# A pre-norm layer in one launch: token rows ahead of code unpacking, the first query step by parts, and the last token block among the feed-forward steps

## The reference, cut to what matters

```python
xn = _layernorm(x)
q = (xn @ Wq + bq).reshape(b, h, t, dh)        # 16 heads of 128
k = (xn @ Wk + bk).reshape(b, t, h, dh).transpose(0, 2, 3, 1)
v = (xn @ Wv + bv).reshape(b, t, h, dh).transpose(0, 2, 1, 3)
weights = softmax(q @ k * scale + causal_mask)
attn = (weights @ v) @ Wo + bo
Wg, Wu, Wd = dequant_nvfp4(...)                # 4-bit codes, a scale per 32 columns
gate, up = xn @ Wg.T, xn @ Wu.T                # 2048 wide
ffn = (gelu(gate) * up) @ Wd.T
return x + attn + ffn
```

## Time and profile before

| | us |
|---|---|
| median of 3 runs | 1270.23 (1269.38 to 1271.47) |
| the profiled execution | 1270.06 |
| its span | 1268.3 |
| PE busy | 1236.2 (97% of the span) |
| DVE busy | 876.2 (69%) |
| ACT busy | 738.6 (58%) |
| POOL busy | 737.8 (58%) |

### The profile page before, as it was taken

One profiled execution on the slowest core, in us unless ns is written; L12 is line 12 of the kernel. 1 busy time (PEld: TensorE's weight loads), 2 busy tenths in 40 slices (PEclk: granted clock), 3 DMA queues, 4 the chain that ended last, 5 costly groups with the idle time before them and its releaser, 6 DMA issues.

```text
span 1268.3 us, 22067 instructions
## 1 busy us (share of the span) xinstructions
PE 1236.2 (97%) x8306; PEld 1119.3 (88%) x8306; DVE 876.2 (69%) x1694; ACT 738.6 (58%) x1533; POOL 737.8 (58%) x772
## 2 busy tenths in 40 slices
PE   8899999999999999999999999999999999999997
PEld 6688888888899999879999998899999879999996
DVE  7687777776577766667667776677667666677765
ACT  3444444444466666657666675566666656666663
POOL 5574455443376676626666663476775527666663
PEclk9999999999999999999999999999999999999999
DMA  5200000000000000110000002010000100000001
GB/s 143 46 14 13 11 10 14 26 2 9 9 26 13 15 13 18 40 49 13 14 26 5 22 13 72 14 55 13 13 22 10 47 26 14 18 22 7 12 5 34
DMA packets 57337, 29.96 MB, mean 24 GB/s; under 512 B 16272, under 2 KB 57232, under 8 KB 57232
## 3 DMA queue, kind: packets, MB, share of 16 engines
q1 hardware_dynamic: 56016, 27.62, 7.9%
q10 hardware_dynamic: 1216, 0.93, 0.2%
HBM read 26.44 MB, written 2.10 MB: 22 GB/s over the span
## 4 chain that ended last, share of the span: by engine, by line
PE 84%; DVE 5%; ACT 4%; POOL 3%; issue 2%; DMA 1%; SPq 1%; ACTq 0%; POOLq 0%; DVEq 0%
PE ps L41 26%; PE ps L43 25%; PE ps L42 25%; PE ps L1029 8%; DVE k_lo L723 2%; ACT k_hi L384 2%; ACT q_all L335 1%; DMA raw<-in_down 1%; PE ps L922 1%; POOL acc L572 1%; DVE pt_lo L770 0%; POOL codes L551 0%; DVE probs L858 0%; DMA wq_in<-in_wq 0%; POOL w_rows L563 0%
## 5 line engine op out<-in xcount | busy, mean ns | idle before, releaser
L635 POOL TENSOR_TENSOR inv_sum<-row_sum,minus_one 128x1 f32<-128x1 f32 x256 | 141.0, 551 | 309.5 <-ACT probs L420 307.7
L638 POOL TENSOR_TENSOR probs<-probs,inv_sum 128x128 f32<-128x128 f32 (+7 forms) x256 | 296.5, 1158 | 20.0
L770 DVE TENSOR_TENSOR pt_lo<-ps,pt_hi 128x512 fp32r<-128x512 f32 (+3 forms) x384 | 204.0, 552 | 97.5 <-ACT pt_hi L406 97.4
L420 ACT ACTIVATE probs<-probs,neg_max 128x128 f32<-128x128 f32 (+7 forms) x256 | 198.1, 774 | 61.2 <-DVE neg_max L858 58.4
L406 ACT ACTIVATE pt_hi<-ps 128x512 fp32r<-128x512 f32 (+3 forms) x384 | 174.2, 489 | 85.2 <-PE ps L1029 85.2
L858 DVE CUSTOM_DVE_ANT_0 probs<-ps,mask_row 128x128 f32<-128x128 f32 (+7 forms) x256 | 192.1, 751 | 2.6
L42 PE MATMUL ps<-pt_lo,v_hi 128*128 128x256 f32 (+1 forms) x640 | 180.1, 281 | 0.0
L43 PE MATMUL ps<-pt_hi,v_lo 128*128 128x256 f32 (+1 forms) x640 | 180.0, 281 | 0.0
L1029 PE MATMUL ps<-ident,probs 128*128 128x128 f32 x1152 | 172.5, 277 | 2.6 <-DVE pt_lo L770 1.9
L41 PE MATMUL ps<-pt_hi,v_hi 128*128 128x256 f32 (+1 forms) x640 | 173.2, 271 | 1.6 <-DVE pt_lo L770 1.6
L618 POOL TENSOR_TENSOR hid_lo<-act_buf,hid_hi 128x512 fp32r<-128x512 f32 x64 | 82.7, 1293 | 147.0 <-ACT hid_hi L359 147.0
(11 more groups left out here) (105 smaller groups left out, 3211.8 us busy)
## 6 DMA issues: line engine op xcount, KB each, us to landing
wq_in<-in_wq SPq DMA_DIRECT2D x63, 128.0 KB, 2.3
kv_in<-in_wk SPq DMA_DIRECT2D x16, 256.0 KB, 2.8
wo_in<-in_wo SPq DMA_DIRECT2D x32, 128.0 KB, 2.0
kv_in<-in_wv SPq DMA_DIRECT2D x32, 128.0 KB, 2.3
out<-acc SPq DMA_DIRECT2D x8, 256.0 KB, 2.6
acc<-in_x SPq DMA_DIRECT2D x2, 512.0 KB, 5.0
raw<-in_gate SPq DMA_DIRECT2D x16, 64.0 KB, 1.8
raw<-in_up SPq DMA_DIRECT2D x16, 64.0 KB, 2.1
```

Of the source, the lines that this page charges most:

```text
L420: nc.scalar.activation(probs[:, s % 4, 0:width], probs[:, s % 4, 0:width], ACT.Exp, bias=neg_max[:, s % 16:s % 16 + 1], scale=-1.0, accum_ ...
L635: nc.gpsimd.tensor_tensor(inv_sum[:, at], row_sum[:, at], minus_one[:], ALU.pow).then_inc(inv_done, 1)
L638: nc.gpsimd.tensor_tensor(row, row, inv_sum[:, at].to_broadcast([P, (i + 1) * P]), ALU.mult).then_inc(probs_done, 1)
L770: nc.vector.tensor_tensor(pt_lo[where], T[at % 2][:, 0:blocks * P].rearrange("p (a b) -> p a b", b=P), pt_hi[where].bitcast(F32), ALU.subt ...
```

## The change

Seven edits, all before the attention stage:

- On DVE `rows(0)` comes ahead of `integers(0)`, with two of the four `bn_stats` of block 1 before it; the other blocks' statistics, rows and integers are spread anew over the query steps.
- On PE `transpose_xn` waits for the rows tile by tile instead of for all four; 86 idle products stand before it and 6 behind it, instead of 96 and 16.
- The first query step, `first_q_step`, makes the eight products that need only the hi halves of the tokens as soon as each is there, then the four with the lo half.
- Block 3 is transposed after feed-forward step 0 instead of after query step 5 (`X_AFTER_F`); blocks 1 and 2 come after query steps 2 and 4, weight chunks 0 and 1 after steps 3 and 5.
- On POOL `make_codes` and `make_rows` of chunks 0 to 2 are spread over the query steps, so `make_rows(2)` comes before the feed-forward loop.
- The bias row is made at k = 9 to 12, and the four `add_bias` run at k = 14, 26, 34 and 46 instead of 0, 2, 4 and 6, behind the sums of one pass over the chunks.
- SP starts the loads in another order: query weights ahead of the packed integers, chunk 2 and 3's integers among them.

```diff
-        X_AFTER_Q = {0: 1, 3: 2, 5: 3}
-        W_AFTER_Q = {4: 0, 6: 1}
+        X_AFTER_Q = {2: 1, 4: 2}
+        W_AFTER_Q = {3: 0, 5: 1}
+        X_AFTER_F = {0: 3}
+        BO_WIDE_AT, BO_ROW_AT = 9, 12
+        ADD_BIAS_AT = {14: 0, 26: 1, 34: 2, 46: 3}
...
             load_x(slice(4, 8), x_in[2])
-            load_raw(0)
-            load_scales(0, 2, first_scales_in, range(4))
             load_q_block(2)
             load_q_block(3)
+            load_raw(0)
+            load_q_block(4)
+            load_q_block(5)
+            load_scales(0, 2, first_scales_in, range(4))
+            load_x(slice(12, 16), x_in[4])
             load_raw(1)
-            load_x(slice(12, 16), x_in[4])
...
             def add_bias(g):
                 pool.wait_ge(bo_row_done, 1)
-                pool.wait_ge(rows_done, 4 * g + 4)
+                pool.wait_ge(acc_done, half_no(g * (TC + 1) + TC, 1))
...
-            if k in (0, 2, 4, 6):
-                add_bias(k // 2)
+            if k in ADD_BIAS_AT:
+                add_bias(ADD_BIAS_AT[k])
...
+            statistics(0, 4)
+            variances(0)
+            statistics(4, 6)
             rows(0)
-            statistics(1)
+            statistics(6, 8)
+            variances(1)
             xn_low(0)
...
             for u in range(8):
                 q_evacuate(0, u)
                 if u == 0:
+                    rows(1)
+                if u == 1:
+                    statistics(8, 12)
+                    variances(2)
+                if u == 2:
                     xn_low(1)
+                    integers(1)
+                if u == 3:
+                    rows(2)
+                    weights_low(0)
+                if u == 4:
+                    statistics(12, 16)
+                    variances(3)
+                    xn_low(2)
+                if u == 5:
+                    integers(2)
+                    weights_low(1)
+                if u == 6:
+                    rows(3)
...
+            def first_q_step():
+                for v in range(2):
+                    pe.wait_ge(wq_lo_done, v + 1)
+                    for ch in range(KC):
+                        pe.wait_ge(xt_hi_done, ch + 1)
+                        for w in (wq_hi, wq_lo):
+                            nc.tensor.matmul(bank_of("Q", 0, 0)[:, v, :], w[:, v, ch, :], xn_hi[:, ch, 0:N],
+                                             start=ch == 0 and w is wq_hi, stop=False)
+                for v in range(2):
+                    for ch in range(KC):
+                        pe.wait_ge(xt_lo_done, ch + 1)
+                        last = nc.tensor.matmul(bank_of("Q", 0, 0)[:, v, :], wq_hi[:, v, ch, :], xn_lo[:, ch, 0:N],
+                                                start=False, stop=ch == KC - 1)
+                    last.then_inc(qp_done, 1)
...
-            idle(96)
+            idle(86)
             pe.wait_ge(ident_made, 1)
             transpose_xn(0)
-            idle(16)
-            pe.wait_ge(xt_lo_done, KC)
+            idle(6)
...
             for k in range(STEPS):
                 gate_up(k)
                 if halves_at(k):
                     down(*halves_at(k))
+                if k in X_AFTER_F:
+                    transpose_xn(X_AFTER_F[k])
```

More of the change, by code:

```diff
@@ L440, in _ @@
                 q_evacuate(0, u)
+                if u == 0:
+                    act.wait_ge(first_scales_in, 64)
+                    nc.scalar.activation(flat(scales[:, 0:2, :]), flat(scales[:, 0:2, :]), ACT.Copy, scale=64.0
+                                         ).then_inc(first_scales_ready, 1)
                 if u in X_AFTER_Q:
@@ L613, in _ @@
                     make_codes(j)
[L614 removed]
+                if k % 4 == 1 and 2 < j < NJ:
                     make_rows(j)
@@ L652, in _, with statistics, variances @@
         def _(dve):
[L653 to L658, removed]
+            def statistics(first, last):
+                for t in range(first, last):
+                    if t in (0, 2) or t >= 4 and t % 4 == 0:
+                        dve.wait_ge(x_in[t // 2 if t < 4 else t // 4 + 1], 16)
                     nc.vector.bn_stats(stats[:, t, :], rows_acc[:, t, :]).then_inc(stats_done, 1)
-                for t in tiles:
+            def variances(g):
+                for t in range(4 * g, 4 * g + 4):
                     dve.wait_ge(stats_done, t + 1)
@@ L776, in o_low, with integers @@
                                                o_hi[:].bitcast(F32), ALU.add, ALU.subtract).then_inc(o_lo_done, 1)
-            statistics(0)
-            for part in range(4):
-                integer(0, part)
+            def integers(j):
+                for part in range(4):
+                    integer(j, part)
+            statistics(0, 4)
+            variances(0)
+            statistics(4, 6)
             rows(0)
-            statistics(1)
+            statistics(6, 8)
+            variances(1)
             xn_low(0)
[L785 to L789, removed]
+            integers(0)
             dve.wait_ge(bq_in, 16)
@@ L907, in transpose_xn @@
             def transpose_xn(g):
-                pe.wait_ge(rows_done, 4 * g + 4)
                 wait(pe, xt_lo_done, KC * g)
-                for b in (2 * g, 2 * g + 1):
-                    for t in range(4):
+                for t in range(4):
+                    pe.wait_ge(rows_done, 4 * g + t + 1)
+                    for b in (2 * g, 2 * g + 1):
                         ch = b % KC
@@ L1059, in _ @@
                     transpose_weights(W_AFTER_Q[u])
-            pe.wait_ge(bo_wide_done, KC)
-            pe.wait_ge(wt_lo_done, 2)
-            for h in range(KC):
-                last = nc.tensor.transpose(M[:, h * P:(h + 1) * P], bo_wide[:, h, :], ident[:])
-            last.then_inc(bo_t_done, 1)
             for k in range(STEPS):
@@ L1070, in _ @@
                     down(*halves_at(k))
+                if k in X_AFTER_F:
+                    transpose_xn(X_AFTER_F[k])
                 if k % 4 == 2 and 2 + k // 4 < NJ:
-                    if k == 2:
+                    if k > BO_ROW_AT:
                         pe.wait_ge(bo_row_done, 1)
                     transpose_weights(2 + k // 4)
+                if k == BO_ROW_AT:
+                    pe.wait_ge(bo_wide_done, KC)
+                    pe.wait_ge(wt_lo_done, 2 + k // 4)
+                    for h in range(KC):
+                        last = nc.tensor.transpose(M[:, h * P:(h + 1) * P], bo_wide[:, h, :], ident[:])
+                    last.then_inc(bo_t_done, 1)
                 run(TAIL.get(k))
```

75 lines of the change are left out of this document (37 added, 38 removed).

## The result

| | before | after |
|---|---|---|
| median, us | 1270.29 (1269.38 to 1271.47, 4 runs) | 1261.26 (1258.61 to 1261.86, 4 runs) |
| ratio | 1 | 0.9921 (95% interval 0.9908 to 0.9933) |
| profiled execution, us | 1270.06 | 1261.86 |
| its span, us | 1268.3 | 1260.1 |

The change is faster by 9.0 us in the medians (8.2 in the profiled executions), well past the 0.2% that can be told. The forecast was 1258.2: the sign and the range were right, the size 3 us too large. The measured 1261.3 lies 1.5 us above the forecast's own case (1256.3 to 1259.8, a chance of 0.66) and where two of its rivals had it, DVE behind (1260.2) and a weaker start (1260.1 to 1261.6).

A forecast was written before the change was run, and what follows sets the result against it. PE, busy 97% of the span, was taken as the bound, leaving its waits and lower clock to gain; -5.6 - 2.7 + 1.0 - 4.6 + 0.0 = -11.9 us gave 1258.2, range 1255.8 to 1262.0.

The forecast's parts named there:

- the forecast's own case: Whole kernel: the summed terms hold and it takes 1256.3 to 1259.8 us; chance 0.66.
- DVE behind: Query steps: rival that DVE's groups are each held 1.0 us by POOL, ending 3.0 after PE's need; 1260.2, chance 0.14.
- a weaker start: Start: rival that block 1's load lands 1.9 us later and the clock may cost 1.5; 1260.1 to 1261.6, chance 0.10.
- end of query step 0: Start: earlier rows and first products let step 0 be issued at 13.8 instead of 19.44, 5.6 us saved.
- query steps 1 to 7: Query steps to first feed-forward product: 23.0 us of PE work instead of 25.7, 2.7 saved, less 1.0 for new waits.
- feed-forward steps 0 to 3: First feed-forward steps: 14.4 us of work instead of 19.4, with 0.4 for a wait at step 4; 4.6 saved.
- later: Later steps: -1.27 for waits gone, +0.88 for waits at two steps, +0.35 for bias-row transposes; 0.0, bounds -1.3 and +1.8.
- its own signs: Sum wrong if rows start after 9.5, PE waits over 2 us in query steps, or clock under 0.9 from 20 us.
- The cover that I gave for the clock: Start: full clock assumed because PE is never idle for more than about half a microsecond from 1.5 us on.
- the 1.0 us for new waits: Query steps: allowance for new PE waits, taken from the 1.01 us wait at 30.37; bounds none or 3 us.
- its six groups: Eight dense steps: DVE's integers 0 to 2 and rows 1 to 3, each held 1.0 us in the DVE rival.
- The rival of the late weight rows: Feed-forward: chunk 2's rows wait for ACT's scales, so the 3.33 and 1.6 us stay; 1263.1, chance 0.04.

The follow-up runs named there:

- second profile after: The changed kernel, nothing altered, timed and profiled again: 0.9919 of the kernel before, 1260.2 us; its profiled execution took 1258.83.
- the start alone: Kernel before with rows of block 0 ahead of the integers, tile-wise transposes, 86 and 6 idle products, first query step by parts; old loads and bias additions: 0.9986.
- the bias additions alone: Kernel before with chunk 2's weight rows ahead of the feed-forward loop and bias additions at k = 14, 26, 34 and 46: 0.9947, 1265.3 us.
- lightened kernel: Changed kernel with POOL's codes and weight rows of chunk 1 cut to 32 of 768 columns, so its result is not the layer's: 0.9894.
- the kernel with the early rows: Changed kernel with the rows of block 2 one place earlier on DVE, ahead of the integers of chunk 1: 0.9905, 1257.5 us.

## Why the prediction was right, and where it was off

| term, us | forecast | first profile after | second profile after |
|---|---|---|---|
| end of query step 0 | -5.6 (13.8) | -3.75 (15.69) | -5.7 (13.76) |
| query steps 1 to 7 | -2.7 + 1.0 | +1.2 (26.90) | +0.15 (25.85) |
| feed-forward steps 0 to 3 | -4.6 | -4.3 (15.11) | -4.2 (15.20) |
| later | 0.0 | -1.3 | -1.5 |
| span | -11.9 | -8.2 | -11.3 |

By its own signs the forecast's sum failed in the middle. The first feed-forward product was to come at 37 to 38 and came at 42.59 and 39.61. PE waited over 2 us within the query steps, and in the first profile the granted clock was 0.50 behind that wait; both were named as signs that the sum is wrong. The waits at steps 4, 17 and 49 and the transposes of chunk 2 came as forecast.

*The start.* In the first profile the load landed 0.6 us later than I took it and the clock was low, the two parts of the rival of the weaker start, in a smaller size; it was priced as one in ten. The cover that I gave for the clock, PE never idle for more than about half a microsecond, did not hold: it was idle for 1.58 us before the first transposes. That rival's cause, the query weights behind the load, finds no support: from issue to landing it took 5.5 to 6.9 us in the eleven profiles with the new order of loads, and with the old one 5.9, 7.0 (the start alone) and 6.7 (the bias additions alone). In the second profile the first product came at 10.90 against 10.85, but that is in part luck. The rows began at 7.95, 0.4 sooner than worked out, and the idle products ran to 9.35, so that the transposes could not follow them.

*The query steps: the step of the prediction that failed is the 1.0 us for new waits.* Over the 23.0 us of work it was 3.9 in the first profile (26.90) and 2.85 in the second. The rival "DVE falls behind" was the true case, by the hold-up and by its size of 3.0: its six groups took 6.4 us longer than at rest in the first profile and 6.1 in the second, where it had 6 (each counted to the start of what follows; at rest 1.08 for integers and 1.28 for rows). Its path was another. It compared DVE's last piece with its date; there PE waited 0.2 us at most. What decided was one group: rows of block 2 beside four POOL instructions without a break, three times their length, with PE waiting for exactly them. The lightened kernel shows the cause, the kernel with the early rows the cure. PE started these transposes 0.4 us late and they cost 2.4 us more than 0.84, (32.17 - 28.96) - 0.84. The low clock behind them cost 1.2 in the first profile: six products took 2.71 us (32.17 to 34.88), and 1.49 in the second (30.10 to 31.59).

*The hold-up that was already there.* That an integer before the change ended as POOL's addition did needs this line of the kernel before beside the earlier trace rows:

```profile
84.41 2.41 POOL L572 TENSOR_TENSOR acc<-acc,bo_row 128x1024 f32<-128x1024 f32 x1
```

The addition ended at 86.82, the integer at 87.05. So the hold-up was known, and the sum took 1.0 for it from the nearest wait.

*The feed-forward steps* came as worked out: the wait of 3.33 us and the low clock behind it went, and 0.46 came at step 4, where I had 0.4. The bias edit alone brought 6.7. The rival of the late weight rows had a part of the truth: `make_rows(2)` did wait 2.42 us for the scales from ACT and ran at 44.44, but PE wanted it only at 51.97.

*The later steps.* Both waits for `w_lo` came, 0.46 each against 0.44, at the two steps named, and from step 4 to the second key projection it took 277.9 us in both. The -1.3 lies behind that, in the attention stage, whose program the change doesn't touch. From there to the end it took 925.8 us before, 924.5 and 924.3 in the two profiles after. Over all profiles it was 924.1 to 926.2, so this is most likely the spread of executions; but the three with the kernel before's order of loads have 925.2 to 926.2, and the others 924.1 to 925.7, and nothing tested whether a part belongs to the change. No term of the forecast had it. It made up for 1.3 of the 4.8 us by which the start and the query steps fell short of the forecast in the first profile, and without it that execution (1261.86) would lie above the range's end of 1262.0. So the number is in the range in part by luck.

*Sum of parts.* I added the terms as shifts of PE. The runs show that they are not free of each other: start alone 1.8, bias alone 6.7, the whole 10.1 by the ratio of 0.9921 on 1271.7; without the early loads of chunks 2 and 3 it falls to 3. That I put the order of loads at nothing was right in the whole, which had it, and wrong as a price of that edit.

## What to carry to other kernels

On an engine that works in order, a gain at the start survives only as far as the next date that something else sets: before counting it, walk along to each later wait and ask whether its releaser has moved too. Where DVE instructions of the kind that waited here (`rows`, `integer`) stand beside an unbroken run of GpSimd's, price each of them with one of the neighbour's, at the place where somebody waits for them, and not the sum over a stage. Moving a long instruction off one neighbour puts it before another: look at who waits for what comes next, two engines on.

## What the runs showed of the hardware

*Row instructions of DVE waited for POOL's one by one.* Four of them took 1.36 us with POOL at rest, 1.77 to 2.89 beside a part of its work, and 4.14 to 4.16 in seven profiles beside the same four POOL instructions in a row. What counts is how long the POOL instruction is that runs when each row is next, and not only that POOL runs without a break: in the kernel with the early rows it did so too, with shorter instructions, and the rows took 2.45. The Trainium skill, page "SBUF — State Buffer", section "SBUF: two separate sides", has an exclusive lock held for a whole instruction; the lightened kernel (4.14 to 2.16 us) agrees with it. Not every DVE instruction waited. Four `bn_stats` took their 1.39 us beside POOL's unbroken work:

```profile
17.47 1.65 POOL L537 TENSOR_TENSOR wq_lo<-wq_in,wq_hi 128x256 fp32r<-128x256 f32 x2 [3.51 <-ACT wq_hi L335]
...
18.68 1.39 DVE L668 BATCH_NORM_STATS2 stats<-acc 128x6 f32<-128x256 f32 x4
...
19.08 1.85 POOL L565 TENSOR_TENSOR codes<-mag,sgn 128x768 int32<-128x768 int32 x1
```

*The clock in the first query step followed the gap before it.* The 86 idle products took between 6.29 and 7.82 us. Where they ended early, PE stood idle longer until the first row tile. Over the profiles of kernels with this start:

| PE idle before the first transposes, us | granted clock, 11.3 to 14.8 us |
|---|---|
| 1.91, 1.58, 1.38 | 0.56, 0.54, 0.53 |
| 1.01, 0.88, 0.71, 0.44, 0.29 | 1.00 in all |
| none (four profiles) | 1.00 in all |

So the clock of the same program came out either way (0.54 and 1.00 in the changed kernel), and a late load and idle products that ended early worked together for the fall. That it fell through the gap and not through something that goes with it was only argued. The three kernels with more idle products (118, 118 and 96) had no gap and kept 1.00, but so did six of the nine profiles with 86. A filler counted in products has no fixed length in time.

*Behind the rows of block 2 the same hold-up left the clock low or not.* In the seven profiles with rows of 4.14 to 4.16 us the mean granted clock from 28 to 36 us was 0.79 in four and 1.00 in three. What decides between them is open.
